# Transformer block with routed experts on one core: last-stage order, one narrow chunk and one attention product moved

## The reference

```
x = x + layernorm(attention(layernorm(x)))
x = x + layernorm(ffn(layernorm(x)))

attention: q, k, v = x @ w.T, 16 heads of width 16
           scores = q k^T / 4, masked causally, except that the first 196
           positions see one another in full; softmax; @ v; @ w_o.T + b_o
ffn:       scores = softmax(x @ gate_w.T); two of 8 experts by scores + gate_b
           expert: a = swiglu((x w1 + b1) * (x w3 + b3)); y = a w2 + b2
           out = sum of the two experts' y, each times its score, + shared expert's y
swiglu(h): g = min(h[even], 7); l = clip(h[odd], -7, 7)
           g * sigmoid(1.702 g) * (l + 1)
```

## Time and profile before

| what | value |
|---|---|
| median of three runs | 2270.2 us |
| the profiled execution's own time | 2272.05 us |
| its span, first to last instruction | 2270.3 us |
| TensorE busy | 2092.2 us, 92% |
| ScalarE busy | 1697.8 us, 75% |
| VectorE busy | 1477.1 us, 65% |
| GpSimd busy | 654.8 us, 29% |
| mean granted TensorE clock | 0.96 |

### The profile page before, as it was taken

The page is one execution under the profiler, slowest core; times in us unless marked ns, Lnnn a source line. Parts: engine busy times, 40 slices in busy tenths (PEclk is TensorE's granted clock), DMA queues, the critical chain, the costliest instruction groups (busy, mean ns, idle before and its releaser), DMA issues. The chain is left out here.

```text
span 2270.3 us, 38461 instructions
## 1 busy us (share of the span) xinstructions
PE 2092.2 (92%) x14097; PEld 1282.3 (56%) x14097; DVE 1477.1 (65%) x2381; ACT 1697.8 (75%) x2165; POOL 654.8 (29%) x648
## 2 busy tenths in 40 slices
PE   7995999999999999999998797999999999999970
PEld 6773333333333333333333796888888888888860
DVE  5663255555555655455555796876788888888865
ACT  5664999999999999999998574333466666666645
POOL 1111000000000000000000343776146566555637
PEclk9997999999999999999999796999999999999985
DMA  6886745555444445555420684564477776667756
GB/s 216 308 295 187 125 61 76 77 74 76 63 61 56 61 67 76 76 74 76 54 42 9 230 274 158 186 244 159 174 220 188 179 198 172 169 173 180 181 171 246
DMA packets 161574, 324.37 MB, mean 143 GB/s; under 512 B 18000, under 2 KB 91856, under 8 KB 155632
## 3 DMA queue, kind: packets, MB, share of 16 engines
q1 hardware_dynamic: 128820, 268.13, 45.9%
q0 software_dynamic: 30256, 46.03, 10.9%
q10 hardware_dynamic: 2316, 7.80, 0.9%
HBM read 198.75 MB, written 127.47 MB: 144 GB/s over the span
## 5 line engine op out<-in xcount | busy, mean ns | idle before, releaser
L1112 ACT ACTIVATE att_prob<-att_scores 128x1024 f32<-128x1024 f32 (+2 forms) x1122 | 997.8, 1031 | 57.5 <-PE att_scores L1059 53.8
L1078 PE MATMUL att_out<-att_prob,att_va 128*32 128x512 f32 (+3 forms) x5000 | 576.8, 542 | 12.5 <-DVE att_prob L1144 12.2
L1059 PEld LDWEIGHTS att_scores<-att_qs,att_ks 50*128 50x128 f32 x2560 | 211.0, 185 | 494.6 <-ACT att_prob L1112 416.7
L1059 PE MATMUL att_scores<-att_qs,att_ks 50*128 50x512 f32 (+3 forms) x2560 | 465.6, 430 | 22.9 <-PEq L118 17.3
L1829 POOL DMA_INDIRECT sums<-moe_y,moe_token x142 | 303.1, 2135 | 256.7 <-ACT moe_y L2113 212.3
L1010 POOL DMA_DIRECT2D ctx_scr<-att_cout x64 | 55.1, 861 | 980.7 <-DVE att_cout L1194 941.7
L1144 DVE SCALAR_TENSOR_TENSOR att_prob<-att_prob,att_tri 128x512 f32<-128x512 f32 x224 | 144.7, 687 | 266.3 <-ACT att_prob L1112 266.3
L1078 PEld LDWEIGHTS att_out<-att_prob,att_va 128*32 128x32 f32 x5000 | 108.8, 108 | 185.5 <-issue 103.3
L1983 PE MATMUL moe_ps<-moe_xt_hi,w_first_hi 128*128 128x512 f32 (+1 forms) x448 | 175.9, 393 | 3.8 <-ACT moe_h L2086 2.1
L1983 PE MATMUL moe_ps<-moe_xt_hi,w_first_lo 128*128 128x512 f32 (+1 forms) x448 | 172.5, 385 | 0.0
L1983 PE MATMUL moe_ps<-moe_xt_lo,w_first_hi 128*128 128x512 f32 (+1 forms) x448 | 172.5, 385 | 0.0
(11 more groups left out here) (295 smaller groups left out, 3930.4 us busy)
## 6 DMA issues: line engine op xcount, KB each, us to landing
qk_parts<-proj_qk SPq DMA_DIRECT2D x64, 512.0 KB, 4.6
keep_first_weights<-w_experts SPq DMA_DIRECT2D x22, 1412.0 KB, 6.7
moe_wraw<-w_experts SPq DMA_DIRECT2D x21, 1412.0 KB, 6.7
att_qs<-qk_parts SPq DMA_DIRECT2D x180, 128.0 KB
att_ks<-qk_parts SPq DMA_DIRECT2D x180, 128.0 KB
moe_rows<-rows_in SPq DMA_DIRECT2D x22, 544.0 KB, 3.9
proj_xin<-x SPq DMA_DIRECT2D x16, 512.0 KB, 3.8
v_scr<-proj_va SPq DMA_DIRECT2D x16, 512.0 KB, 3.5
```

The source lines that it names most:

```text
L1059: last = nc.tensor.matmul(pss[e % SBUFS][:, h, at:at + CH - q0], ks[s][rows, half, kt * P:(kt + 1) * P], qs[s][rows, half, c * CH + q0:(c ...
L1078: last = nc.tensor.matmul(pso[k % 2][strip, q0:], va[team % 2][:, kt, strip], probs_of(u)[:, h, at:at + CH - q0], start=(kt == 0), stop=(i ...
L1112: nc.scalar.activation(probs_of(u)[:, half * 2:half * 2 + 2, start:], pss[e % SBUFS][:, :, start:], ACT.Exp, scale=HD ** -0.5)\
```

## The change

Three things change in the last stage, one in the experts' chunk order, one in attention.

- VectorE does `measure(0)` before the result of the last chunk instead of after it.
- VectorE, not GpSimd, adds `y` to the last pair's sums, and VectorE does the very last add of x1, with a semaphore of its own (`last_chunk_ready`) for the store.
- SyncE issues the loads sums(7), x1(4), sums(6), x1(5), x1(6), x1(7) in a row, and then all stores.
- The last narrow chunk is routed chunk 38 (the last one) instead of 36.
- The late unit's product stands behind that of unit 30 instead of 33, and VectorE's steps end after unit 30 instead of 32; three of them move to units 21, 23 and 24.

```
-NARROW_AT = (4, 9, 15, 20, 25, 31, 36)
+NARROW_AT = (4, 9, 15, 20, 25, 31, 38)

-LATE_STEPS = {13: 1, 14: 2, 15: 2, 16: 2, 17: 1, 25: 2, 26: 1, 27: 2, 28: 1, 29: 2, 30: 1, 31: 2, 32: 1}
-LATE_USED = NU - 3
+LATE_STEPS = {13: 1, 14: 2, 15: 2, 16: 2, 17: 1, 21: 1, 23: 1, 24: 1, 25: 2, 26: 1, 27: 2, 28: 1, 29: 2, 30: 1}
+LATE_USED = NU - 6

 GpSimd
-                    if p == last - 1:
-                        pool.wait_ge(acc_loaded[last], 2 * 16)
-                        for i in range(2):
-                            c = NEC - 2 + i
-                            pool.wait_ge(y_biased[c % 2], c // 2 * 2 + 2)
-                            nc.gpsimd.tensor_tensor(acc[last][i], acc[last][i], y[c % 2][:], ALU.add)\
-                                .then_inc(y_added, 1)
                     ...
+                    if p == last:
+                        break

 SyncE
                 def store(p):
                     sp.wait_ge(first_done, p + 1)
-                    sp.wait_ge(second_done, p + 1)
+                    if p < PAIRS - 1:
+                        sp.wait_ge(second_done, p + 1)
+                    else:
+                        sp.wait_ge(last_done, 1)
...
-                for p in range(EARLY, PAIRS):
-                    if p >= EARLY + 2:
-                        load_sums(p)
+                load_sums(PAIRS - 1)
+                load_x1(EARLY)
+                load_sums(EARLY + 2)
+                for p in range(EARLY + 1, PAIRS):
                     load_x1(p)
-                    if p >= EARLY + 1:
-                        store(p - EARLY - 1)
-                for p in range(PAIRS - EARLY - 1, PAIRS):
+                for p in range(PAIRS):
                     store(p)

 VectorE
                     if p == PAIRS - 1:
+                        c = NEC - 2 + i
+                        dve.wait_ge(y_biased[c % 2], c // 2 * 2 + 2)
+                        V.tensor_tensor(acc[p][i], acc[p][i], y[c % 2][:], ALU.add).then_inc(y_added, 1)
                         dve.wait_ge(y_added, i + 1)
...
                     if nxt is None:
+                        measure(0)
                         result(n, s)

                 in_turn(NEC, step)
-                measure(0)
                 for p in range(PAIRS):
                     invert(p)
                     if p + 1 < PAIRS:
                         measure(p + 1)
+                last = PAIRS - 1
+                dve.wait_ge(x1_loaded[last], 2 * 16)
+                dve.wait_ge(normed, PAIRS * PT)
+                V.tensor_tensor(acc[last][1], acc[last][1], x1[last][1], ALU.add).then_inc(last_done, 1)
```

More of the change, by code:

```diff
@@ L1740, in experts @@
         first_done, second_done = ph.sem("first_chunks_ready"), ph.sem("second_chunks_ready")
+        last_done = ph.sem("last_chunk_ready")
         HALF = FIRST // 2
```

## The result

The changed kernel takes 2256.7 us (median of 5 runs, 2254.7 to 2262.5) against 2270.2 (5 runs, 2267.2 to 2270.8): ratio 0.9949, 95% interval 0.9937 to 0.9960, or 9 to 14 us less (11.6 in the middle; the two medians differ by 13.5). The forecast was 2259.7. The profiled execution took 2254.69 us (span 2253.0), 17.4 us less than the one of before.

What follows compares the result with a forecast made beforehand. ScalarE's exponentials bound attention; the last stage is a relay of VectorE, ScalarE and GpSimd. Terms 4.2 + 0 + 6.3 = 10.5 us, from 2270.2 to 2259.7; range 2255.5 to 2265.

Steps and rivals of the forecast that it cites:

- Attention: Late product behind unit 30: next team starts earlier, 0.32 us at each of 14 boundaries, less team 15's loss: 4.2 us.
- the walk: Stepping through engine starts: in attention, next team 0.23 to 0.46 us earlier; in the last stage, the order of adds.
- team 15: Attention's last team with a late unit: has the new wait of 0.3 us and no boundary to gain.
- Late probability in time: Attention: VectorE's moved steps end near 392.9, before TensorE needs the late probability; margin 2.1 us.
- rival 4: Attention: the late product waits for VectorE; 1 us beyond the margin costs 15, giving 2279; chance 0.03.
- Narrow chunk: Experts: last routed chunk narrow is worth 0, +-1.0 for both ends; the sums' loads go out 3.7 us or more earlier.
- Statistics first: Head of last stage: measure(0) runs ahead of the result, so invert(0) starts 4.97 us earlier, as does the relay behind.
- Loads ahead of stores: Last stage: eleven loads in a row, then stores; both directions hidden, worth 0.
- The last adds: End of last stage: y adds and closing add on VectorE; closing add ends at 2258.15, tail gain 6.3 us in all.
- rival 3: Last stage: VectorE first both times (8.7), or adds do not exclude each other (10.4); 2255.6 to 2257.3; chance 0.09.
- VectorE's add comes in the same moment: Last stage: VectorE's first y add meets GpSimd's start of pair 5's second add at 2240.72.
- the middle order: Last stage: GpSimd first at one of the two adds, given by two of four orders; tail gain 6.3 us.

Runs made afterwards that it cites:

- after: The changed kernel with all edits, against the kernel before: 2256.7 us against 2270.2, ratio 0.9949.

## Why the forecast held, step by step

**Attention, forecast 4.2, measured 2.6 (3.0 by the run with it alone).** The mechanism was right, and the new wait at unit 33 too: by starts it costs 0.48 us, as the walk had it; its bracket shows 0.19. By starts, a team in the middle of the stretch gains 1.06 at the boundary and pays 0.27 at unit 1, 0.04 at unit 3 and 0.48 at unit 33, in all 0.26 (64.29 to 64.03) but for rounding. So 0.32 was taken where 0.26 came: 14 x 0.06 = 0.8 too much. That it was so near is luck in part. The next team's first exponential comes 1.06 - 0.48 = 0.58 sooner, more than the walk's 0.23 to 0.46, because TensorE's last round takes 1.44 us (401.13 to 402.57) and not 1.60 or more; and the walk left out the wait at unit 1, though the earlier trace rows show it, and charged 0.06 for what costs 0.27 + 0.04. The second mis-sized term is team 15, put at -0.3: it came out 0.63 longer (63.37 to 64.00), as it pays at units 1, 3 and 33 and gains no boundary. Its 0.3 counted unit 33 alone, and by "in ends it is nearer 0.28" for 0.48. A bracket starts at the end of a record that overlaps the next one (1.21 long at a distance of 0.90), so it is some 0.3 short of what the wait costs. The last 0.4 are passing waits that differ in a few teams, above all 3 and 4, and that the regular pitch does not have.

**Late probability in time.** Margin 2.1 forecast, 2.14 measured; the lateness of rival 4 did not arise.

**Narrow chunk.** 0 forecast, 0 within 0.1 us. The loads of the sums left 10.35 us before the last a_lo's end instead of 6.44: the 3.9 met "3.7 or more".

**Statistics first.** 4.97 forecast, 5.19 measured; without it the last add is 4.6 later (there the second result half came 0.45 us sooner than in after).

**Loads ahead of stores.** 0 forecast, 0.1 measured, and 0.02 from the first reciprocal on.

**The last adds, the term that was mis-sized.** The forecast was 57.1 us, the run 54.16. VectorE got in first at both adds, which the forecast had as part of rival 3 (8.7; measured 9.3, of which 0.2 is the earlier reciprocal and 0.4 is not placed). Its step that failed is "VectorE's add comes in the same moment", with the middle order taken; with it fell the sign that ScalarE's 7.36 before the last root becomes "7 or a little more": it became 4.47. The order is not chance: in after and in all eight other runs with these adds VectorE is 0.04 to 0.08 us ahead. VectorE's add starts 0.09 before the shift's record ends (2232.38 against 2232.30 + 0.17). The walk left this overlap out: 2245.75 less 0.09 is just ahead of GpSimd's 2245.69. By the walk's own figures GpSimd was 0.06 us ahead: a term that hangs on such a tie, worth 5.0, 6.3 or 8.7, should have carried the orders evenly, and VectorE first had only rival 3's 0.09. That two errors of opposite sign (1.6 too much, 3.0 too little) met in the sum is why 10.5 was near 11.9: luck, and not the walk.

## What to carry to other kernels

Where two engines exclude each other, plan the order of starts, not the sum of times: keep the slower engine's long instructions apart wherever the faster one has a chain of short dependent steps, because every long one can cost the chain a whole wait (2.26 us for a step of 0.17 here). What is won at the head of a relay of engines without slack arrives at its end in full; moving a long instruction off the relay onto an idle engine is no gain if it runs back to back with others there. Price a wait from start to start, not by its idle bracket, when the records overlap; and cut a product along the dimension that TensorE streams, not along heads that it does side by side.

## What the runs showed of the hardware that was not expected

A matmul of four heads, each on its own strip of 32 partitions, takes as long as one of two heads: 0.97 and 0.96 us for 512 columns, 0.55 for 256. GpSimd's adds of 128x1024 back to back (2.3 apart) let one VectorE instruction with two SBUF operands through at each boundary, and three such instructions in a chain took 0.74, 2.26 and 2.26 us where each takes 0.17 alone; the reciprocal and the batch-norm statistics beside the same adds kept their time (0.20, and 1.41 for four beside an add against 2.70 for eight away from them). In the output projection the same 900 matmuls took 152.3 to 160.5 us over fourteen traces, with TensorE's granted clock at 0.87 to 0.80.
